# First cross attention: which engine makes the context's low halves in the weighted sum, and in which order ScalarE serves the scores

## What is computed

```python
q   = layernorm(x) @ (wq.T @ wk) * scale      # 512 x 512
s   = q @ context.T                           # 512 x 8192, the scores
p   = softmax(s, axis=-1); p = where(mask == 0, 0, p)
o   = p @ context                             # 512 x 512, the weighted sum
out = project(o @ wv.T) + proj_b
```

## Time and profile before

| | us |
|---|---|
| median of 3 runs | 1198.41 (1198.33 to 1198.84) |
| the profiled execution, its own time | 1201.41 |
| its span, first to last instruction | 1199.7 |
| PE busy | 1055.1 (88%) |
| DVE busy | 861.4 (72%) |
| ACT busy | 486.1 (41%) |
| POOL busy | 375.0 (31%) |
| mean granted clock of TensorE | 0.930 of full speed |

### The profile page before, as it was taken

The page is one execution under the profiler, slowest core; times in us unless marked ns, Lnnn a source line. Parts: engine busy times, 40 slices in busy tenths (PEclk is TensorE's granted clock), DMA queues, the critical chain, the costliest instruction groups (busy, mean ns, idle before and its releaser), DMA issues.

```text
span 1199.7 us, 14437 instructions
## 1 busy us (share of the span) xinstructions
PE 1055.1 (88%) x4788; PEld 490.7 (41%) x4788; DVE 861.4 (72%) x1180; ACT 486.1 (41%) x730; POOL 375.0 (31%) x173
## 2 busy tenths in 40 slices
PE   7999999699999879879638899999889879886897
PEld 3444444344444334434313344444622144464353
DVE  5577777799999337485974299999467448475795
ACT  2354544566666147225771210100034515335163
POOL 4245545243444044000001277776100020182003
PEclk9999999799999889879969899999969989998897
DMA  6144544533221457311010245455100100000000
GB/s 241 54 151 155 181 146 149 194 105 105 93 85 67 166 187 264 119 41 47 1 71 0 93 177 195 179 194 142 36 1 1 41 32 1 1 2 1 1 1 35
DMA packets 41827, 112.60 MB, mean 94 GB/s; under 512 B 4512, under 2 KB 15296, under 8 KB 35648
## 3 DMA queue, kind: packets, MB, share of 16 engines
q1 hardware_dynamic: 38592, 101.13, 24.1%
q10 hardware_dynamic: 2880, 9.96, 2.5%
q0 software_dynamic: 320, 1.05, 0.3%
HBM read 103.18 MB, written 7.34 MB: 92 GB/s over the span
## 4 chain that ended last, share of the span: by engine, by line
PE 57%; DVE 23%; issue 9%; ACT 7%; DMA 1%; DVEq 1%; ACTq 0%; SPq 0%; POOL 0%; POOLq 0%
PE PS L1549 5%; PE PS L1551 5%; PE PS L1550 5%; PE PS L249 4%; PE PS L250 4%; PE PS L251 4%; DVE arena L666 3%; PE PS L1617 3%; DVE XN L616 2%; DVE arena L1840 2%; PE PS L751 2%; PE PS L752 2%; PE PS L753 2%; PE PS L1595 2%; DVE arena L669 1%
## 5 line engine op out<-in xcount | busy, mean ns | idle before, releaser
L721 PE MATMUL PS<-arena 128*128 128x512 f16 x256 | 97.1, 379 | 9.7 <-POOL arena L468 7.6
L493 POOL TENSOR_TENSOR arena<-arena 128x2048 f16<-128x2048 f32 x16 | 70.8, 4427 | 110.5 <-ACT arena L538 104.5
L751 PE MATMUL PS<-arena 128*128 128x512 f16 x256 | 97.9, 383 | 5.8 <-DVE arena L666 5.8
L1549 PE MATMUL PS<-arena 128*128 128x512 f16 x256 | 97.0, 379 | 1.8 <-DVE arena L1434 1.8
L752 PE MATMUL PS<-arena 128*128 128x512 f16 x256 | 98.0, 383 | 0.0
L753 PE MATMUL PS<-arena 128*128 128x512 f16 x256 | 97.8, 382 | 0.0
L722 PE MATMUL PS<-arena 128*128 128x512 f16 x256 | 97.0, 379 | 0.0
L723 PE MATMUL PS<-arena 128*128 128x512 f16 x256 | 97.0, 379 | 0.0
L1550 PE MATMUL PS<-arena 128*128 128x512 f16 x256 | 97.0, 379 | 0.0
L1551 PE MATMUL PS<-arena 128*128 128x512 f16 x256 | 97.0, 379 | 0.0
L666 DVE SCALAR_TENSOR_TENSOR arena<-arena,MASK 128x512 f16<-128x512 f16 (+1 forms) x64 | 95.6, 1494 | 0.3
(11 more groups left out here) (356 smaller groups left out, 2347.3 us busy)
## 6 DMA issues: line engine op xcount, KB each, us to landing
arena<-in_ctxT SPq DMA_DIRECT2D x32, 1024.0 KB, 6.4
arena<-in_ctx SPq DMA_DIRECT2D x16, 1024.0 KB, 5.3
arena<-in_w ACTq DMA_DIRECT2D x8, 1024.0 KB, 5.1
arena<-in_w SPq DMA_DIRECT2D x8, 1024.0 KB, 4.8
XN<-in_ffnGU SPq DMA_DIRECT2D x16, 384.0 KB, 3.3
XN<-in_WinT SPq DMA_DIRECT2D x16, 290.0 KB, 5.0
gu_hi<-arena SPq DMA_DIRECT2D x16, 192.0 KB, 3.3
gu_lo<-arena SPq DMA_DIRECT2D x16, 192.0 KB, 3.5
```

The lines of the kernel that those rows point to most:

```text
L721: pe.matmul(bank, CHI[:, b, e, cols], QHI[:, e, :], start=(e == 0), stop=False)
L751: pe.matmul(PS[:, t, :], PHI[:, j, cols], CHI[:, b, j, :], start=False, stop=False)
L1549: pe.matmul(bank, QHI3[:, e, cols], CHI3[:, b, e, :], start=(e == 0), stop=False)
```

## The change

On POOL the loop that made `CLO` in the weighted sum is gone, but for chunk 0. DVE makes `CLO` of chunks 1 to 15 itself (`s0_row_low`), behind the first tile of the same chunk. At the start of the weighted sum DVE shifts three tiles instead of four (and instead of five before its first low half), waits there for the spills, and takes each sum of chunk 0 one tile later. In the scores ACT copies all four tiles of a chunk first, then makes `chunk_hi`, and only then `turned_hi`.

```diff
-            with pool.Fori(0, PAIRS) as i:
-                for b in range(2):
-                    c = i * 2 + b
-                    pool.wait_ge(s0_c_hi, c + 1 + AHEAD_SPLIT)
-                    settle(pool)
-                    pool.tensor_tensor(CLO[:, b], CR[:, b], CHI[:, b], ALU.subtract).then_inc(s0_c_lo, 1)
+            pool.wait_ge(s0_c_hi, 1 + AHEAD_SPLIT)
+            pool.tensor_tensor(CLO[:, 0], CR[:, 0], CHI[:, 0], ALU.subtract).then_inc(s0_c_lo, 1)
...
-            def s0_take(c, half, b):
+            def s0_take(c, b):
                 for j in range(CH):
                     k = c * CH + j
                     act.wait_ge(s0_scores, k + 1 + AHEAD_TILES)
                     act.activation(ST[:, k, :], PS[:, b * CH + j, :], ACT.Copy).then_inc(s0_copied, 1)
-                    if j == 2:
-                        turned_hi(c, half, b)
...
-                    s0_take(i * 2 + b, i, b)
+                    s0_take(i * 2 + b, b)
                     chunk_hi(i * 2 + b + 2, b, i * 16 + 32)
+                    turned_hi(i * 2 + b, i, b)
                     round_raw(i * 2 + b + 1, 1 - b)
...
-            for s in s2_spill:
-                dve.wait_ge(s, (PAIRS + 1) * SPILLED)
             dve.wait_ge(pe_marks, PE_MARK["s0_spread"])
...
+            def s0_row_low(c, b):
+                dve.wait_ge(s0_c_hi, c + 1 + AHEAD_SPLIT)
+                settle(dve)
+                dve.tensor_tensor(CLO[:, b], CR[:, b], CHI[:, b], ALU.subtract).then_inc(s0_c_lo, 1)
+
+            def s0_chunk_low(c, b, ahead):
                 for j in range(CH):
                     k = c * CH + j
                     if ahead:
                         s0_shift_tile(k + CH)
...
+                    s0_tile_low(k, j)
+                    s0_tile_sum(k)
+                    if j == 0:
+                        s0_row_low(c, b)
+
+            for j in range(3):
+                s0_shift_tile(j)
+            for s in s2_spill:
+                dve.wait_ge(s, (PAIRS + 1) * SPILLED)
             for j in range(CH):
-                s0_shift_tile(j)
-            with dve.Fori(0, PAIRS - 1) as i:
+                s0_tile_low(j, j)
+                if j:
+                    s0_tile_sum(j - 1)
+                s0_shift_tile(j + 3)
+            s0_shift_tile(2 * CH - 1)
+            s0_tile_sum(CH - 1)
+            s0_chunk_low(1, 1, True)
+            with dve.Fori(0, PAIRS - 2) as i:
                 for b in range(2):
-                    s0_chunk_low(i * 2 + b, True)
-            s0_chunk_low(NCH - 2, True)
-            s0_chunk_low(NCH - 1, False)
+                    s0_chunk_low(i * 2 + 2 + b, b, True)
+            s0_chunk_low(NCH - 2, 0, True)
+            s0_chunk_low(NCH - 1, 1, False)
```

More of the change, by code:

```diff
@@ L553, in s0_act @@
                 for b in range(2):
-                    s0_take(i * 2 + b, i, b)
+                    s0_take(i * 2 + b, b)
                     chunk_hi(i * 2 + b + 2, b, i * 16 + 32)
+                    turned_hi(i * 2 + b, i, b)
                     round_raw(i * 2 + b + 1, 1 - b)
-            s0_take(NCH - 2, PAIRS - 1, 0)
+            s0_take(NCH - 2, 0)
+            turned_hi(NCH - 2, PAIRS - 1, 0)
             round_raw(NCH - 1, 1)
@@ L560, in s0_act @@
             act.activation(CHI[:, 0], CR[:, 0], ACT.Copy).then_inc(s0_c_hi, 1)
-            s0_take(NCH - 1, PAIRS - 1, 1)
+            s0_take(NCH - 1, 1)
+            turned_hi(NCH - 1, PAIRS - 1, 1)
             act.activation(COLS[:, 44:45], EPSC[:, 0:1], ACT.Exp)
@@ L655, in s0_shift_tile, with s0_tile_low, s0_tile_sum @@
                 dve.tensor_tensor(ST[:, k, :], ST[:, k, :], SPREAD, ALU.subtract).then_inc(s0_shift, 1)
-            def s0_chunk_low(c, ahead):
+            def s0_tile_low(k, j):
+                dve.wait_ge(s0_p_hi, k + 1)
+                dve.wait_ge(s0_pv, k + 2)
+                settle(dve)
+                dve.scalar_tensor_tensor(out=PLO[:, j, :], in0=ST[:, k, :], scalar=MASK[:, bass.ds(k, 1)],
+                                         in1=PHI[:, j, :], op0=ALU.mult, op1=ALU.subtract).then_inc(s0_p_lo, 1)
+            def s0_tile_sum(k):
+                dve.wait_ge(s0_sum, k + 1)
+                dve.tensor_tensor(PSUMS, PSUMS, ST[:, k, :], ALU.add).then_inc(s0_sum, 1)
+            def s0_row_low(c, b):
+                dve.wait_ge(s0_c_hi, c + 1 + AHEAD_SPLIT)
+                settle(dve)
+                dve.tensor_tensor(CLO[:, b], CR[:, b], CHI[:, b], ALU.subtract).then_inc(s0_c_lo, 1)
+            def s0_chunk_low(c, b, ahead):
                 for j in range(CH):
@@ L662, in s0_chunk_low @@
                         s0_shift_tile(k + CH)
[L663 to L669, removed]
-            for j in range(CH):
-                s0_shift_tile(j)
-            with dve.Fori(0, PAIRS - 1) as i:
+                    s0_tile_low(k, j)
[6 more added lines that the diff above has]
+                dve.wait_ge(s, (PAIRS + 1) * SPILLED)
+            for j in range(CH):
+                s0_tile_low(j, j)
[6 more added lines that the diff above has]
+            with dve.Fori(0, PAIRS - 2) as i:
                 for b in range(2):
-                    s0_chunk_low(i * 2 + b, True)
-            s0_chunk_low(NCH - 2, True)
-            s0_chunk_low(NCH - 1, False)
+                    s0_chunk_low(i * 2 + 2 + b, b, True)
+            s0_chunk_low(NCH - 2, 0, True)
+            s0_chunk_low(NCH - 1, 1, False)
             dve.wait_ge(pe_marks, PE_MARK["s0_den"])
```

## The result

The changed kernel takes **1187.97 us** (median of 4 runs, 1186.04 to 1189.38), against 1198.62 of the kernel before, run beside it (1198.33 to 1202.09): a ratio of 0.990, 95% interval 0.988 to 0.992. Faster by 1%, clear of the noise, and inside the range, but 4.4 us over the predicted time. The profiled execution took 1188.89, its span 1187.2.

What follows compares the result with a forecast made beforehand. Scores: DVE and ACT chasing each other, 11.28 us a turn against PE's 10.345; weighted sum: DVE held off by POOL, 3.23 a chunk. Terms -9.3 - 1.5 - 0.5 - 3.5 = -14.8: 1201.4 to 1186.6, median 1183.6; range 1179 to 1191.5.

Steps and rivals of the forecast that it cites:

- ScalarE's order, scores: Scores: ACT's new order ends ten PE waits of 0.93 us for POOL's low half; -9.3 us, bounds 0 and -9.3.
- the turn between the loops, PE's wait: Between the loops: PE's wait for the last maximum falls from 5.4 to 3.0-3.1 us; taken as -1.5, bounds 0 and -3.5.
- head of the weighted sum: Start of weighted sum: three subtractions instead of five before the first low half; -0.5 us, bounds 0 and -1.2.
- weighted sum: Weighted sum: low half on DVE takes 2.28 us, DVE's chunk 9.73, under PE's 10.345; -3.5 us, bounds +17 and -3.5.
- its last step: Whole kernel: from the profiled execution's 1186.6 us to the runs' median, taken to stand 3.0 lower, 1183.6.
- VectorE was full of its own work: Rival, weighted sum: the 3.97 us is the instruction's own, not POOL's doing, so the kernel gets slower, 1221 us; chance 0.04.
- the lag from the transfer eats part: Turn between the loops: lag from the raw chunk's transfer reduces the -2.3 us gain, so -1.5 is taken.
- The circle: Scores: transpose, SP's issue, transfer (6.4 us), `chunk_hi`, POOL, `turned_lo`, DVE: 21.0 us for two chunks against PE's 20.7.
- POOL's 3.2 us of slack: Scores: POOL's low half is done some 3.2 us before PE wants it, covering about 2 us of transfer lag.
- the transfer paces the scores: Rival, scores: at 7.5 us to landing a chunk takes 11.05, 6 of the 9.3 and the turn's gain lost; 1191; chance 0.20.
- The clock's rival: Rival, turn: PE idles too briefly for its clock to fall, saving 2.2 us and half the turn's slow products; 1180; chance 0.08.

Runs made afterwards that it cites:

- e5: The changed kernel with VectorE writing the low half of chunks 1 to 15 of the weighted sum twice, same values; 1211.68 us, ratio 1.010.
- e3: The changed kernel with SyncE issuing spills and the next raw chunk ahead of its wait for the transpose; 1183.91 us, ratio 0.987.
- e7: The changed kernel with SyncE's raw chunk issued ahead of the transpose wait and VectorE making chunk 0's low half between the loops; 1182.86 us, ratio 0.986.

## Why the prediction was right, and where it was off

In the profiled executions the forecast was -14.8 and -12.5 came out. Term by term, predicted and measured:

| term | predicted | measured |
|---|---|---|
| ScalarE's order, scores | -9.3 | -8.2 |
| the turn between the loops, PE's wait | -1.5 | +1.0 |
| head of the weighted sum | -0.5 | -0.4 |
| weighted sum | -3.5 | -3.4 |

(Turn: 5.4 to 6.4. Head: from PE's transposes to the first product, 222.88 to 231.82 before, 215.66 to 224.20 after. Scores: the last product of the stage starts at 217.1 before and at 208.9 after; 0.2 of this is an earlier start of the stage.) These make -11.0, the lead at the last product of the weighted sum (402.8 to 391.8). The profiled pair gains 1.5 more behind it, in stages whose code the change doesn't touch. In the ten traces, from the last product of the weighted sum to the end, the three kernels with the old weighted sum take 796.4 to 797.1 and the seven with the new one 793.6 to 795.2; whether that is the change's doing is not shown.

On the medians, with -10.7, the prediction missed 4.4: the terms are 3.8 short, the 1.5 behind them come off, and 2.1 are its last step. It took the profiled execution to stand 3.0 over the runs, as before the change; the changed kernel's stands 0.9 over. (The 1.7 that an execution takes outside its span is in every run and is no part of the 3.0.)

**The weighted sum** went as worked out: 2.29 for the instruction where 2.28 was taken from two rows of other sizes, no low half held, DVE under PE. The rival "VectorE was full of its own work" is out: the 3.23 went whole, and e5 shows what a chunk costs once DVE is over PE's time. The Trainium skill's page "SBUF — State Buffer", section "Who interferes with whom", gives the mechanism, an exclusive lock; these rows agree in either direction (below).

**The scores** went as worked out in mechanism, but for the two late waits for POOL: 48 products in the window, `turned_lo` (L622) behind POOL, and DVE's 24-element instruction at 0.18 in place of 1.31. `turned_lo` takes 3.47 in the mean of 15, near the 3.5 said, though it goes from 2.4 to 4.3 where it meets POOL.

**The step that failed is the turn**, "I take -1.5", and in it the size of the lag: "the lag from the transfer eats part". The circle was right in its members, and one of them was too small: the 6.4 to landing is the median over the whole run. Within this loop the median is 6.6, in the kernel before as in the changed one, and the loads that ACT waited for took 6.9 in the mean to `chunk_hi`'s start. The 0.5 is the difference between the 21.0 worked out for two chunks and the 21.5 measured (twice 10.74). That is 0.4 a chunk over PE, not 0.15. POOL's 3.2 us of slack covered it for nearly the whole stage, with 1.0 of PE lost ahead of the last chunk and 0.4 two chunks earlier. The lag then stood at the turn in full: counted from the start of PE's last chunk (198.75), the transpose of the piece before ends at 204.63, at S+5.9 where S+2.7 was worked out, and PE's wait is 6.4 where 3.0 to 3.1 was worked out, 3.2 and 3.3 late. In e3, without the lag, both come out as reckoned: the transpose ends at S+2.8 (199.88, with S at 197.1) and the wait is 3.3. So of the rival "the transfer paces the scores" a good part came true: the turn's gain is gone and 1.3 of the scores', not the 6 that a landing of 7.5 each time would have taken.

**The clock's rival** is not tested at its price: no run here keeps the higher level through the whole turn. In e3 and e7, where PE's wait is shorter, its transposes do run at the higher level (last section), but behind the second wait the first products of the weighted sum are at the lower one again.

Not settled: why the transfers take the 6.3 to 7.6 that they take there. In the changed kernel the weights' piece, two spills and the raw chunk go out within 2 us; in e3 the weights' piece goes out 4 us behind the chunk, which lands in 4.9. Which of the neighbours slows it was not tried. Nor is it settled why the lag at the turn differs from execution to execution (5.9, 5.9, 5.4 and 4.7 in four kernels with the same scores).

## What to carry to other kernels

Before moving work off an engine that is busy all the time, look at whether its instructions are longer beside another engine's than alone; here bringing the other engine's work over was the cure. When a circle of waits is broken, work out the next longest circle with the durations that its transfers have at their place in the queue, not with a median over the run, and follow the lag to the end of the loop: slack hides it from the bounding engine until the loop ends, and the turn pays all of it at once. Then cut the second circle too: e3's reorder alone gave nothing, and on top of the change 4 us.

## What the runs showed of the hardware

The hold between VectorE and GpSimd works both ways. In the changed kernel's scores POOL's subtraction starts while DVE's multiplication runs, and is the longer one: 4.77 where 4.08 is usual, 0.69 more, with 0.82 of it before DVE's end at 160.83.

```profile
159.00 1.83 DVE L613 SCALAR_TENSOR_TENSOR XN<-XN 128x768 f32<-128x768 f32 x1
...
160.01 4.77 POOL L468 TENSOR_TENSOR arena<-arena 128x2048 f16<-128x2048 f32 x1
```

And PE's four transposes at the turn ran at both levels of its clock in these runs. After a wait of 6.4 us (the changed kernel) and of 3.3 (e3), ns min/median/max:

```profile
L752 PE MATMUL PS<-IDENT,arena x4: 421/421/447, 215.7 to 216.3; 128*128 128x128 f32 x4
```

```profile
L754 PE MATMUL PS<-IDENT,arena x4: 272/272/302, 210.9 to 211.3; 128*128 128x128 f32 x4
```

In e7, after 1.65, the spread behind them runs at the higher level too (granted 1.00 from 210 to 213, 0.50 from 216 to 224 in the changed kernel), but after the 4.9 us that follow, the first products are at the lower level again, with 0.56 granted from 217 to 224. In e7 the short wait was worth little for the clock, since a longer one came next.

```profile
210.00:213.00 3.00, 2.52 (x16) 1.49 (x15) 2.94 (x4) 1.07 (x2) 0.00 (x0) 1.00 0.53 149
217.00:224.00 7.00, 6.62 (x18) 2.44 (x19) 6.90 (x12) 6.15 (x9) 0.00 (x0) 0.56 0.71 269
```

```profile
216.00:224.00 8.00, 4.57 (x16) 2.54 (x14) 4.14 (x8) 2.63 (x6) 0.00 (x0) 0.50 0.80 259
```
